# Last layer of a four-layer graph network: another order of units and of the steps within a period, turned halves in two banks

## The reference, cut to what matters

```python
sub = _mobius_add(-x, y, c)
sub_norm = norm(sub)
log_ij = 2.0 / (sqrt_c * lam_x) * arctanh(clip(sqrt_c * sub_norm)) * sub / sub_norm
w = adj / deg
agg = einsum('ij,ijc->ic', w, log_ij)
x = _layernorm(x + _expmap(0, agg @ weight + bias))
```

## Time and profile before

| | |
|---|---|
| median of 3 runs | 1581.26 us (1580.57 to 1583.12) |
| the profiled execution | 1582.32 us, of it a span of 1580.5 us |
| busy in the span | PE 1392.8 us (88%), PEld 603.8 (38%), DVE 1235.0 (78%), ACT 930.4 (59%), POOL 213.2 (13%) |
| sums of the 72 units (line 2413) | 72 of them, 1122.7 to 1523.4 us |
| edge weighting (line 727) | 72 of them, 170.8 us, 2372 ns each |

### The profile page before, as it was taken

How to read it: one execution, slowest core, us unless ns; L and a number is a source line. 1 busy time by engine, 2 the same in 40 slices (tenths; PEclk the granted TensorE clock), 3 DMA queues, 4 the chain that set the end, 5 groups by cost and what they waited for, 6 DMA issues and landing times. The chain is left out here.

```text
span 1580.5 us, 20433 instructions
## 1 busy us (share of the span) xinstructions
PE 1392.8 (88%) x7857; PEld 603.8 (38%) x7882; DVE 1235.0 (78%) x1623; ACT 930.4 (59%) x888; POOL 213.2 (13%) x145
## 2 busy tenths in 40 slices
PE   4999999789978699999999999979988898888870
PEld 1433333223324244454454454534433333333330
DVE  4899866676785877968969958528688878999877
ACT  0000286358633555445456456766879989989964
POOL 1000000000000000000000001223224444444430
PEclk9999999999997799999999999989869989999995
DMA  9999599979999255434434432234534546455600
GB/s 332 409 409 409 233 407 410 413 286 409 409 414 411 76 189 216 179 134 181 180 120 180 184 117 67 79 108 158 176 103 137 179 150 204 148 181 179 213 15 27
DMA packets 135896, 348.93 MB, mean 221 GB/s; under 512 B 7732, under 2 KB 57208, under 8 KB 135544
## 3 DMA queue, kind: packets, MB, share of 16 engines
q1 hardware_dynamic: 119968, 329.27, 56.0%
q10 hardware_dynamic: 15832, 18.36, 3.3%
HBM read 329.78 MB, written 17.83 MB: 220 GB/s over the span
## 5 line engine op out<-in xcount | busy, mean ns | idle before, releaser
L955 PE MATMUL ps<-ring,X 128*64 128x512 f32 x512 | 263.8, 597 | 15.2 <-DVE ring L2149 15.2
L956 PE MATMUL ps<-work,X 128*64 128x512 f32 x512 | 263.8, 597 | 0.0
L1471 ACT ACTIVATE work<-ring 128x2048 f32<-128x2048 f32 x64 | 122.3, 1911 | 156.4 <-PE ps L963 122.9
L963 PE MATMUL ps<-work 128*64 128x512 bf16 x768 | 208.2, 380 | 0.0
L961 PE MATMUL ps<-work 128*64 128x512 bf16 x768 | 208.2, 380 | 0.0
L727 POOL TENSOR_TENSOR ring<-ring,work 128x1024 f32<-128x1024 f32 x72 | 170.8, 2372 | 247.7 <-DVE work L2406 247.7
L824 PE MATMUL ps<-ring,work 128*64 128x512 f32 x672 | 159.5, 620 | 20.7 <-DMA ring<-in_adjT 20.7
L720 POOL TENSOR_SCALAR work<-ring 128x1024 int16<-128x1024 uint8 x24 | 27.0, 1127 | 1031.8 <-DMA ring<-codes 930.7
L961 PEld LDWEIGHTS ps<-work 128*64 128x64 bf16 x768 | 84.7, 110 | 177.4 <-issue 151.9
L1131 PE MATMUL ps<-ident,work 128*128 128x128 f32 x448 | 79.8, 305 | 52.5 <-DVE work L2338 26.0
L1297 ACT ACTIVATE work<-work,code_bias 128x2048 uint8<-128x2048 bf16 (+1 forms) x32 | 62.3, 1947 | 90.6 <-DVE work L1892 80.2
(11 more groups left out here) (365 smaller groups left out, 2847.2 us busy)
## 6 DMA issues: line engine op xcount, KB each, us to landing
ring<-in_adjT SPq DMA_DIRECT2D x88, 2048.0 KB, 15.9
work<-in_adjT SPq DMA_DIRECT2D x28, 2048.0 KB, 20.0
ring<-in_adjT SPq DMA_DIRECT2D x24, 1024.0 KB, 9.7
ring<-in_adjT SPq DMA_DIRECT2D x48, 512.0 KB, 3.8
ring<-codes SPq DMA_DIRECT2D x32, 512.0 KB, 3.7
ring<-in_adjT SPq DMA_DIRECT2D x64, 256.0 KB, 3.0
codes<-work ACTq DMA_DIRECT2D x32, 256.0 KB, 6.1
codes<-work ACTq DMA_DIRECT2D x64, 128.0 KB, 1.8
```

The costliest lines, as they stand in the source:

```text
L955: nc.tensor.matmul(ps[0:F, h, :], rows, ring[:, r, k, cols], start=start, stop=stop)
L956: nc.tensor.matmul(ps[F:P, h, :], rows, negs[:, pair, i, cols], start=start, stop=stop)
L963: mm = nc.tensor.matmul(ps[F:P, 2 + h, :], part, less[:, pair, i, cols], start=start and t == 0, stop=stop and t == 2)
L1471: nc.scalar.activation(negs[:, pair], ring[:, s % RING, 2 * pair:2 * pair + 2, :], ACT.Relu, scale=-1.0).then_inc(negs_made, 1)
```

## The change

ORDERS now goes quarter by quarter: all units whose later quarter is I stand in the string of I, O, I and D units mixed. All gathers add in bank 4, with one `first` and one `last` unit for each quarter, and `add_direct` runs one period earlier, in period n for unit n-2. The freed bank 5 takes the second half of a turned unit, so that both turns of unit n-1 stand together in period n, and both mirror weights behind the sum of n. On VectorE the product of n+1 moves ahead of the sum of n, and the two adds stand between the weight of n-1 and this product. On ScalarE the logarithm of n stands ahead of the angle of n-1, and the raise of n+1 ahead of the root of n. On TensorE the push of n+1 stands in period n behind the products. `move_x` does its eight blocks at once in bank 6 (it was bank 5 or 7 and two halves in two periods), in periods 14, 18, 20 and 29, and `keep_moved` follows at the end of the same VectorE period. The third piece of `turn_flips` goes from period 10 to 9.

From ORDERS and the code that plans the products follow, for the changed kernel: `add_mirror` in periods 13, 15, 17, 25, 30, 34, 36, 42, 47, 52, 56, 58, 64, 68 and 72; `add_direct` in 7, 21, 43 and 73; periods between 12 and 71 without products 17 to 20, 25, 36, 37, 42, 47, 58 and 59; four products in 12, 13 and 14, two in the others.

```diff
@@ -216,7 +216,7 @@
...
-        ORDERS = ["OOODOODODOODIIOODOOD", "OOOODIDIOOODODOOOO", "OOOODIDIOOOOOOOO", "OOOODIDIOOOOOOOODD"]
+        ORDERS = ["DDDDII", "OODOOIIDOOODOD", "OOOOOOOODIDIOOOODOOOOD", "OOOOOOOODIDIOOOOOOOOOOOOOOOODD"]
@@ -247,31 +247,16 @@
...
+            left = {"O": [(J, I, k) for J in range(I) for k in range(CB)], "I": [(I, I, k) for k in range(2)],
+                    "D": [(I, I, k) for k in range(GB)]}
+            assert all(order.count(kind) == len(left[kind]) for kind in left)
+            for i, kind in enumerate(order):
+                u = Unit(len(units), kind, *left[kind].pop(0))
+                u.first, u.last = i == 0, i == len(order) - 1
                 units.append(u)
-        for stream in (off_units, own_units):
-            for u, before, after in zip(stream, [None] + stream, stream[1:] + [None]):
-                u.first = not before or before.I != u.I
-                u.last = not after or after.I != u.I
-        ends = [u for u in units if u.last]
-        for stream in (off_units, own_units):
-            done = 0
-            for u in stream:
-                u.kept_before = done
-                if u.last:
@@ -290,11 +275,11 @@
...
-        MOVED_AT = [6] + [u.n + 3 for u in own_units if u.last and u.I < NQ - 1]
         LAST_AT = 8
-        FLIP_AT, FLIPS_OUT_AT = (26, 2, 10), (28, 3, 10)
-        assert not units[FLIP_AT[2] - 2].turned
-        FLIP_TURNS = sum(u.turned for u in units[0:FLIP_AT[2] - 2])
+        FLIP_AT, FLIPS_OUT_AT = (26, 2, 9), (28, 3, 10)
+        assert not units[FLIP_AT[2] - 1].turned
+        FLIP_TURNS = sum(u.turned for u in units[0:FLIP_AT[2] - 1])
+        MOVES_AT = [u.n + 1 for u in units if u.kind == "D" and u.n > LAST_AT + 4][0:NQ]
@@ -1101,36 +1085,36 @@
...
+                if n == 0:
+                    wait_for_copies(COPIED[3])
+                for c in range(CB):
                     b = n * CB + c
-                    mm = nc.tensor.matmul(ps[:, bank, c * F:(c + 1) * F], UT[0:F, b * P:(b + 1) * P], w3_sb[:],
+                    mm = nc.tensor.matmul(ps[:, 6, c * F:(c + 1) * F], UT[0:F, b * P:(b + 1) * P], w3_sb[:],
                                           start=True, stop=True)
-                if CB - 1 in blocks:
-                    mm.then_inc(moved_made, 1)
-
-            def turn_g(u, h):
-
-                if h == 0:
-                    pe.wait_ge(g_made, u.n + 1)
...
+                pe.wait_ge(g_made, u.n + 1)
+                moves = sum(n <= u.n for n in MOVES_AT)
+                if moves:
+                    pe.wait_ge(moved_kept, moves)
+                for h in range(2):
+                    if u.offs:
+                        pe.wait_ge(mirror_weighted, 2 * u.offs - 1 + h)
+                    elif h == 0:
+                        pe.wait_ge(sum2_copied, 2 * NQ)
+                    else:
+                        pe.wait_ge(signs_copied, FLIPPED[2])
+                    if u.offs == FLIP_TURNS:
+                        pe.wait_ge(signs_copied, FLIPPED[3])
+                    for c in range(GB):
+                        mm = nc.tensor.transpose(ps[:, 6 - h, c * P:(c + 1) * P],
+                                                 u.angle[:, (h * GB + c) * P:(h * GB + c + 1) * P], ident[:])
+                    mm.then_inc(g_turned, 1)
 
             def gather(u):
 
@@ -1138,20 +1122,17 @@
...
                     wait_for_copies(3)
-                if u.first and not u.off and not u.I:
-                    pe.wait_ge(signs_copied, FLIPPED[2])
-                if u.first and u.kept_before:
-                    pe.wait_ge(direct_added, u.kept_before)
-                if u.first and not u.off and u.I:
-                    pe.wait_ge(moved_kept, u.I + 1)
+                if u.first and u.I:
+                    pe.wait_ge(direct_added, u.I)
                 for h, b in enumerate(u.rows):
                     if u.off:
-                        mm = nc.tensor.matmul(ps[h * F:(h + 1) * F, u.sums, :], points[:, b, :],
-                                              u.edges[:, h * HALF:(h + 1) * HALF], start=u.first, stop=u.last)
+                        mm = nc.tensor.matmul(ps[h * F:(h + 1) * F, 4, :], points[:, b, :],
+                                              u.edges[:, h * HALF:(h + 1) * HALF], start=u.first, stop=u.last,
+                                              skip_group_check=True)
                         continue
                     for t in range(2):
                         cols = slice(u.targets[h] * 2 * P, (u.targets[h] + 1) * 2 * P)
-                        mm = nc.tensor.matmul(ps[t * F:(t + 1) * F, u.sums, cols], points[:, b, :],
+                        mm = nc.tensor.matmul(ps[t * F:(t + 1) * F, 4, cols], points[:, b, :],
                                               u.edges[:, h * HALF + t * 2 * P:h * HALF + (t + 1) * 2 * P],
                                               start=u.first and h == 0, stop=u.last and h == 1, skip_group_check=True)
@@ -1183,36 +1164,31 @@
...
                     distances(units[0])
+            push_apart(units[0])
             for n in range(LAST_PERIOD):
-                if unit_at(n):
-                    push_apart(units[n])
                 if unit_at(n + 1):
                     distances(units[n + 1])
-                if n - 1 in MOVED_AT:
-                    move_x(MOVED_AT.index(n - 1), range(GB, CB))
-                if n == FLIP_AT[2]:
-                    turn_flips(2)
-                if turned_at(n - 2):
-                    turn_g(units[n - 2], 1)
                 if unit_at(n - 2):
                     gather(units[n - 2])
                 for quad, c in products[n]:
                     mirror_products(quad, c)
+                if unit_at(n + 1):
+                    push_apart(units[n + 1])
                 if turned_at(n - 1):
-                    turn_g(units[n - 1], 0)
-                if n in MOVED_AT:
-                    move_x(MOVED_AT.index(n), range(GB))
+                    turn_g(units[n - 1])
+                if n in MOVES_AT:
+                    move_x(MOVES_AT.index(n))
                 if n in (LAST_AT, LAST_AT + 2):
                     turn_last_nodes((n - LAST_AT) // 2)
-                if n == FLIP_AT[1]:
-                    turn_flips(1)
+                if n in FLIP_AT[1:]:
+                    turn_flips(FLIP_AT.index(n))
@@ -1610,15 +1586,16 @@
...
             for n in range(LAST_PERIOD):
-                v = unit_at(n - 1)
-                if v:
-                    act.wait_ge(sum_made, v.n + 1)
-                    nc.scalar.activation(v.angle, v.angle, ACT.Ln, scale=2.0 / DIST_SCALE).then_inc(
-                        angle_made, 1)
-                u = unit_at(n)
+                u, v = unit_at(n), unit_at(n - 1)
                 if u:
                     act.wait_ge(prod_made, u.n + 1)
                     nc.scalar.activation(u.log, u.log, ACT.Ln, bias=TINY_PROD, scale=1.0).then_inc(log_made, 1)
+                if v:
+                    act.wait_ge(sum_made, v.n + 1)
+                    nc.scalar.activation(v.angle, v.angle, ACT.Ln, scale=2.0 / DIST_SCALE).then_inc(angle_made, 1)
+                if unit_at(n + 1):
+                    raise_dist(units[n + 1])
+                if u:
                     if u.n >= 3:
                         act.wait_ge(weighted, u.n - 2)
                         w = units[u.n - 3]
@@ -2335,7 +2310,7 @@
...
-                V.tensor_tensor(folded[u.quad % 2][few][:, :, u.cols[h]], ps[:, 6, :].rearrange("p (b c) -> p b c", c=P),
+                V.tensor_tensor(folded[u.quad % 2][few][:, :, u.cols[h]], ps[:, 6 - h, :].rearrange("p (b c) -> p b c", c=P),
@@ -2364,7 +2339,7 @@
...
-                add_sums(2 * u.I, HALF, ps[:, u.sums, :]).then_inc(direct_added, 1)
+                add_sums(2 * u.I, HALF, ps[:, 4, :]).then_inc(direct_added, 1)
@@ -2393,19 +2368,19 @@
...
-                v = unit_at(n - 3)
-                if v and v.last:
-                    add_direct(v)
-                if n - 1 in products_end[:-1]:
-                    quad = products_end.index(n - 1)
-                    add_mirror(quad, units[quad_ends[quad]])
                 v = unit_at(n - 1)
                 if v:
                     dve.wait_ge(angle_made, v.n + 1)
                     dve.wait_ge(inv_made, v.n + 1)
                     V.scalar_tensor_tensor(v.angle, v.angle, ANGLE_CLIP, v.log, ALU.min, ALU.mult).then_inc(g_made, 1)
-                if turned_at(n - 2):
-                    mirror_weights(units[n - 2], 0)
+                w = unit_at(n - 2)
+                if w and w.last:
+                    add_direct(w)
+                if n - 1 in products_end[:-1]:
+                    quad = products_end.index(n - 1)
+                    add_mirror(quad, units[quad_ends[quad]])
+                if unit_at(n + 1):
+                    multiply(units[n + 1])
                 u = unit_at(n)
@@ -2414,10 +2389,11 @@
...
-                    mirror_weights(units[n - 2], 1)
```

(34 more changed lines are left out.)

34 lines of the change are left out of this document (5 added, 29 removed).

## The result

The changed kernel takes **1624.2 us** (median; 1620.6 to 1626.8) against 1580.9 (1577.5 to 1583.1): 1.027 times the time before, 95% interval 1.0244 to 1.0305. The profiled execution took 1626.8 us, its span is 1625.1, 44.6 more than before. So the kernel became slower, 9 us more than the forecast said and within its range.

The account below looks back on a forecast made before the run. Bound: a ring through VectorE, TensorE and ScalarE, 4.79 us a period. 59 periods: 282.6 + 57.5 (25 lost races) + 10 (small parts) = 350.1 against 316.4; 1581.3 + 33.7 = 1615 us, range 1572 to 1668.

Parts of the forecast that it names:

- The ring: Chain of waits through VectorE, TensorE and ScalarE, 9.58 us over two periods: 4.79 a period, 282.6 us for 59 periods.
- The race: VectorE's product and GpSimd's edge weighting both read SBUF; the later start waits for the earlier; product ahead by 0.17 us.
- rival 1: The product never waits for GpSimd's edge weighting, so the short ring prevails: 1564 us; chance 0.14.
- rival 2: Each lost race idles TensorE, its clock falls, distances is late, the next race is lost: 1677 us; chance 0.13.
- The price: Cost of one race the product loses to edge weighting: a period of 6.99 instead of 4.79, put at 2.3 us.
- The count: Lost races in 59 periods: 16 by adds, 7 carried on by TensorE's clock, 2 by four products; 25 together, 57.5 us.
- 16 add periods: 14 mirror and 2 direct adds between weight and product start it at 1.46 or later, behind edge weighting's 1.30: all lost.
- 7 named followers: Periods behind add periods without products: TensorE waits 3.1 us, its clock falls, distances is late, 7 more races lost.
- 2 losses by four-product periods: Periods 12 to 14 have four products, 14 a move_x too, making TensorE over 1 us late: 2 more lost races.
- margin of 0.12: When ScalarE has waited for the sum, product starts at sum + 3.51, edge weighting at + 3.63: product wins by 0.12 us.
- small parts: move_x 0.7 to 1.6, make_scales and norm_rows 2.3 together, half-clock periods with products some 5: 10 us, from 5 to 15.
- Rival 3: Balance: some 11 lost races cancel the gain, small parts near their lower bound: 1581 us; chance 0.06.

Follow-up runs that it names:

- experiment 10: Changed kernel plus, from the twelfth period on, a VectorE copy of 256 PSUM columns to SBUF between the adds and the product: 1684.5 us.
- experiment 5: Changed kernel with both adds moved to the start of VectorE's period, ahead of the weight (direct add one period later): 1567.2 us, 0.9918.
- experiment 9: Changed kernel plus one 128x512 memset on VectorE between the adds and the product, in periods 12 to 71: 1623.6 us.

## Why the prediction was right, and where its terms were off

**The ring** of 4.79 us is shown: the 26 short periods with a product average 4.79 (4.64 behind a lost one, 4.92 next), and with the raise moved back the period is 5.34 for 5.33 worked out. (ScalarE's five starts by its mean of 0.94 make 4.70 and not 4.72, a slip that changes nothing.)

**The race** is shown from both ends: decided by order (1566.4) or without reads (1566.6) the time is that of rival 1, 1564; with a sure loss each time it is near rival 2's 1677 (1684.5). The changed kernel lies between, as argued. What decides is where the product starts relative to GpSimd. The mechanisms of the two rivals are another matter: the product was not spared in the changed kernel, and in experiment 10 a copy makes each loss, so that run prices losses in every period and does not show them feeding themselves. The Trainium skill says ("SBUF — State Buffer", Who interferes with whom) that issue order decides who blocks; by that rule the product that is ahead by 0.02 to 0.03 (experiment 5) keeps its time, and the one at 0.06 behind (below) does not, and both traces agree. Experiment 9, where a product 0.38 behind is not held up, fits only if the memset ahead of it counts as the first.

**The price** of a lost race was put at 2.3 us. Its terms don't give that: 6.99 less 4.79 is 2.20, and the deduction makes it smaller still. The long periods average 7.19, 2.40 above the ring, so 2.3 was near by a slip that went the right way. The 0.2 us above 6.99 are not evenly spread: 20 of the 31 lie between 6.99 and 7.14, and 15 and 55 have 8.26 and 7.90, because distances starts 2.57 and 2.36 us behind the sum there.

**The count** was the term that was off, 31 for 25. All 16 add periods came out long, and all 7 named followers (18, 19, 26, 37, 38, 48, 59). The 2 losses by four-product periods did not come (period 14 is 4.64); TensorE's lateness from period 14 went into period 15, lost to its add anyway. In the add periods 13, 15, 30, 34, 52, 56, 64 and 68, which have products, TensorE waits at most 1.6 us and distances keeps 1.13, as the prediction took it to. Eight came that were not in the list: 20 and 60, a further period at the lower clock, and 22, 27, 39, 44, 55, 61, each behind a period in which TensorE has products to do and much of it at the lower clock. Timeline of period 22:

```profile
1269.79 1.22 DVE L2388 SCALAR_TENSOR_TENSOR work<-ps,work 128x1024 f32<-128x1024 f32 x1
...
1270.32 1.09 PE L1115 MATMUL ps<-ident,work 128*128 128x128 f32 x8
...
1271.35 1.13 PE L1072 MATMUL ps<-work 64*128 64x512 f32 x4
...
1272.22 1.22 DVE L2375 SCALAR_TENSOR_TENSOR work<-work,stage_words 128x1024 f32<-128x1024 f32 x1
...
1273.52 2.37 POOL L712 TENSOR_TENSOR ring<-ring,work 128x1024 f32<-128x1024 f32 x1 [4.83 <-DVE work L2375]
1273.58 3.39 DVE L2303 SCALAR_TENSOR_TENSOR turn_in<-turn_in 128x1024 f32<-128x1024 f32 x1
```

TensorE had spent the period before mostly at the lower clock with products to do (granted clock 0.59 from 1264.0 to 1271.3), and turns until 1271.4. Distances, now at full speed, starts 1.56 us behind the sum instead of 1.29. The weight too is 0.10 later than 2.33 behind the sum. Of the margin of 0.12 remains 0.12 - 0.27 + 0.10 = -0.05, and the product is 0.06 behind. The prediction saw these full periods ("half-clock periods with products fill TensorE beyond 7 us: some 5") and booked them as 5 us of small parts; their worth was another lost race each, six of the eight. That is the step that failed. In 21 and 43 the period was long as predicted but by another way: the direct add waited until 1267.98 for a gather at the lower clock (1.97 us), and the product started at edge weighting's end (1268.65 against 1268.69) and took 1.22: no race was lost there.

**The sum again with measured terms:** 282.6 + 31 x 2.40 = 74.4, less 27 x 0.05 = 1.3 (all of it from the last period, 3.57), and 1.5 for the one period of 6.30, is 357.2. Against the predicted 350.1 that is +16.9 for the races and -9.8 for the small parts: what was booked as 10 us of small parts does not appear beside the long periods. Of the 16.9, 13.8 come from the count and 3.1 from the price. That the two misses cancel in good part, and the time comes out 9 us off, is luck. Kernels without the race (292.8 to 301.8) show that small parts exist: they lie 10 to 19 us above 282.6, adds included.

**First twelve periods:** 83.6 us for 84.3, booked at 0. **Tail:** 1 us for 0.

Rival 3 (balance by few losses) fell with the 16 add periods. What stays open: why the start of the stage differs by up to 6 us between kernels with the same code up to there; and how much of the fall to the lower clock would be avoided by other work for TensorE, since the only work tried left periods of 8.2 us next to it.

## What to carry to other kernels

Where two engines read SBUF in a way in which the later one waits, write down for every period who starts first and by how much. Here a margin of 0.17 us decided about 58 us in a 1.6 ms kernel, and a 0.4 us add in the wrong place used it up. Put the order down as a wait on the engine that has slack rather than leave it to a race: here its instruction then starts 1.2 us later and ends 0.25 us later, and no small instruction elsewhere can turn the order round. Before moving an add, ask who waits for its bank.

## What was not expected of the hardware

- The race is decided within a few hundredths: a product 0.02 to 0.03 us ahead keeps 1.23 us (experiment 5), one 0.06 behind takes 3.39.
- A memset of 128x512 floats, without inputs, 0.03 ahead of GpSimd's multiplication was followed by a product that was not blocked though it started 0.38 behind it, while GpSimd took 3.77 us (experiment 9). A copy from PSUM in the same place did not have this effect (experiment 10). That the memset held GpSimd off and the product took over from it without a gap is the reading that fits; it was not measured alone, and period 27 with the same recorded starts went the other way.
- In the add periods without products a lost race leaves TensorE waiting 3.2 to 4.2 us ahead of distances (3.20 at 1294.81), which then takes 2.08 instead of 1.13, and the next race is lost or the period is long all the same. After the waits of 1.6 us in add periods with products it keeps 1.13.
